# Attention products on four column tiles in a decoder block, and self maxima over 32 queries of four chunks

## The chip, the cores and the metric

The program runs on one core of one Trainium2 chip. The metric is the device time of one execution in microseconds (us), the median of some runs. TensorE (PE in the profile) multiplies; its weight loads are listed as PEld. VectorE is DVE, ScalarE is ACT, GpSimd is POOL, and SP only issues transfers.

## What is computed

A pre-norm decoder block on `x` of 4 x 1024 tokens with 256 features: windowed self attention (16 heads of 16, chunks of 128 queries that see their own chunk causally and the whole chunk before), cross attention over 77 context rows, and a gated layer with fake quantized operands.

```python
x = x + _L0_attn_ref(_layernorm(x, axis=-1), L0_attn_w_qkv, L0_attn_w_out)
x = x + _L0_xattn_ref(_layernorm(x, axis=-1), ctx_1024, ctx_1024, mask_SxS2_ik0, ...)
x = x + _L0_ffn_ref(_layernorm(x, axis=-1), L0_ffn_clip_x, ...)
```

Inside the self attention (`k_prev` of the first chunk is zeros, and those keys are masked out):

```python
scores = jnp.einsum('bhcqd,bhckd->bhcqk', qc, kcat) / HD ** 0.5
causal = wq[:, None] + W >= jk[None, :]
scores = jnp.where(mask[None, None], scores, -jnp.inf)
attn = jax.nn.softmax(scores, axis=-1)
```

## The kernel before

The attention is cut into 16 jobs (four batches x self `s` or cross `x` x half of the heads), each of two groups `g` of four heads: 32 groups. Jobs alternate along the list `JOBS`. All engines walk one list of steps, `attention_order()`: the steps of several jobs are interleaved by a table of places (`PLACE`, fractions of a group's length `LENGTH`) and by how many steps a follower stands behind (`BEHIND`). The order is fixed when the program is built, and the change leaves it as it is. A step uses one or two of six PSUM banks in a ring (`banks_of`); PE waits at a step until the engine that reads the banks' former content is done. Two more banks, `acc`, take the value products.

The steps, by the names that the diff uses:

- `turned`: eight transposes of normalized tokens (`xn`, f32), to `xnT` by ACT.
- `qk`: queries (z = 0) and keys (z = 1) of 512 tokens, f32. ACT and DVE split them into three bf16 parts, and SP copies the parts to `qs` and `ks` (96 rows: six products of parts for 16 features).
- `v` and `xkeys`: values of self and cross attention, f32.
- `max`: raw scores with the queries as weights, so that DVE can take each query's maximum over the keys (`tensor_reduce` with negation into `mneg`). For self attention a step is one chunk `c` of 128 queries against 256 keys (the chunk before and its own), four heads, and a product with `identb` and `causal` adds the mask. A group has eight such steps; for c = 0 there are only 128 keys. For cross attention a step is two chunks against 77 keys, with `maskq` as the mask.
- `rows` and `turnm`: DVE splits the maxima into three bf16 rows, PE transposes them, ACT copies them out (`m3t`) and sends them into rows 96 to 98 of `qs`, where the score product subtracts them.
- `score`: the scores again with the keys as weights, 128 keys by up to 256 queries, 99 rows; ACT takes the exponential into `pt`, and for self attention POOL zeroes what is not causal.
- `val`: values as weights (17 columns: 16 features and a one for the sum), f32, four heads side by side on four column tiles of 32, before and after the change.
- `out`: the output projection, f32.

An f32 matmul of the program stands twice in the trace: it is run as two.

From about 735 us on the gated layer runs, with full-width products; it is not touched.

The lines of the full-width products that the change replaces are L610, L630, L640, L649, L667 and L670 (self maxima), L677 and L679 (cross maxima), L687, L699 (self scores), L706 and L709 (cross scores), and L759. Transposes (L589, L595, L618, L771, L776) stay full width. L737 and L748 are the value products.

## Time and profile before

| | before |
|---|---|
| median of three runs | 855.02 us (847.9 to 858.87) |
| span of the profiled execution | 849.0 us |
| PE busy | 684.6 us, 5391 matmuls |
| DVE busy | 545.8 us |
| ACT busy | 415.1 us |
| POOL busy | 188.8 us |
| granted TensorE clock, mean over the span | 0.91 |

The profiled execution is one execution; its span, from the first to the last instruction, stands beside the runs' median, which is 6.0 us more. Busy times are shares of that span; PE's include the modelled latency of each matmul, so that what PE really does in a stretch is better read from the starts of its matmuls. A row of the timeline merges like instructions that follow each other: its first number is the start of the first, the second the time in which they are busy, and the count stands at the end. A matmul's form, such as 96*128 96x256 bf16, says 96 rows and 128 columns of weights, and 256 columns streamed.

### The profile page before, as it was taken

Reading aid. Unit: us, or ns where it says so; the run is one execution under the profiler, and the core shown is the slowest. Engines: PE = TensorE matmul, PEld = TensorE weight load, DVE = VectorE, ACT = ScalarE, POOL = GpSimd, SP = SyncE. Lnnn points to the kernel's source line nnn. Section 1 sums busy time; section 2 is a strip of 40 time slices with the busy share of each in tenths; the row PEclk is TensorE's granted clock in tenths of the full one; section 3 lists DMA queues with packets and bytes.
Section 4 is the critical chain, followed back from the end, with each engine's and each line's share of the span. In section 5 each row is a group of like instructions: output and inputs, shape, how many; then the busy total and the mean of one; then the engine's idle time right before and its main releaser. Section 6 shows DMA issues by size and latency. Waiting matters only on the chain.

```text
span 849.0 us, 14814 instructions
## 1 busy us (share of the span) xinstructions
PE 684.6 (81%) x5391; PEld 414.9 (49%) x5396; DVE 545.8 (64%) x975; ACT 415.1 (49%) x610; POOL 188.8 (22%) x231
## 2 busy tenths in 40 slices
PE   2579999989996998999979989897886784488565
PEld 1346565655653564556644644464543442233254
DVE  6277658866864456677636874556745651679996
ACT  2324665536463444555334446433343352399775
POOL 5002131312231120310113123002002000044436
PEclk9988999999997997999988989997998786699989
DMA  7534243502622153243222432331237112000013
GB/s 215 125 106 143 54 128 81 149 3 90 165 77 61 21 170 105 46 141 78 86 50 96 109 96 69 97 95 42 70 85 211 23 42 53 0 1 2 0 65 135
DMA packets 59557, 71.83 MB, mean 85 GB/s; under 512 B 25003, under 2 KB 36447, under 8 KB 59487
## 3 DMA queue, kind: packets, MB, share of 16 engines
q1 hardware_dynamic: 53391, 68.01, 29.2%
q10 hardware_dynamic: 6096, 2.88, 1.3%
q8 instruction: 44, 0.72, 0.4%
q14 instruction: 26, 0.21, 0.1%
HBM read 17.74 MB, written 4.72 MB: 26 GB/s over the span
## 4 chain that ended last, share of the span: by engine, by line
PE 49%; DVE 22%; issue 8%; ACT 7%; SPq 6%; DMA 6%; ACTq 1%; POOL 1%; POOLq 0%; DVEq 0%
PE banks L630 8%; PE banks L759 7%; PE banks L667 5%; PE banks L737 5%; DVE mneg L1179 4%; PE banks L699 4%; PE banks L640 3%; PE banks L748 3%; SPq L523 3%; PE banks L670 3%; DVE xn L1143 2%; SPq L517 2%; PE banks L706 2%; PE banks L709 2%; DVE tops L1358 2%
## 5 line engine op out<-in xcount | busy, mean ns | idle before, releaser
L1179 DVE TENSOR_REDUCE mneg<-banks 128x4 f32<-128x1024 f32 (+1 forms) x128 | 145.1, 1151 | 68.0 <-PE banks L670 67.5
L974 ACT ACTIVATE big<-banks 128x1024 f32<-128x1024 f32 (+1 forms) x128 | 123.0, 974 | 105.4 <-PE banks L699 101.7
L1451 POOL TENSOR_SCALAR_AFFINE_SELECT big<-big 128x512 f32<-128x512 f32 x128 | 83.1, 650 | 391.6 <-ACT big L974 390.9
L978 ACT ACTIVATE big<-banks 77x1024 f32<-77x1024 f32 x64 | 65.3, 1020 | 86.3 <-PE banks L709 81.8
L667 PE MATMUL banks<-big 96*128 96x256 bf16 (+1 forms) x512 | 94.5, 280 | 13.4 <-DMA big<-parts 9.8
L630 PE MATMUL banks<-xnT,weights 128*128 128x512 f32 x192 | 92.9, 617 | 3.9 <-ACT big L978 3.9
L699 PE MATMUL banks<-big 99*128 99x256 bf16 (+1 forms) x512 | 79.3, 280 | 13.3 <-DMA big<-m3t 5.7
L1183 DVE TENSOR_REDUCE mneg<-banks 128x8 f32<-128x616 f32 x64 | 50.3, 793 | 57.7 <-PE banks L679 57.6
L737 PE MATMUL banks<-big 128*17 128x256 f32 (+1 forms) x1152 | 79.0, 366 | 1.0 <-POOL big L1451 0.6
L670 PE MATMUL banks<-causal,identb 128*128 128x256 bf16 x256 | 72.9, 288 | 0.0
L667 PEld LDWEIGHTS banks<-big 96*128 96x128 bf16 x512 | 47.9, 103 | 45.9 <-issue 26.6
L699 PEld LDWEIGHTS banks<-big 99*128 99x128 bf16 x512 | 45.0, 101 | 48.3 <-issue 32.5
L803 PE MATMUL banks<-oe,weights 128*128 128x512 bf16 x187 | 46.8, 394 | 11.0 <-DVE big L1352 4.4
L630 PEld LDWEIGHTS banks<-xnT,weights 128*128 128x128 f32 x192 | 35.7, 197 | 38.1 <-issue 31.4
L677 PE MATMUL banks<-big 96*128 96x77 bf16 x512 | 43.1, 214 | 13.2 <-DMA big<-kparts 9.6
L706 PE MATMUL banks<-big 99*77 99x256 bf16 x256 | 51.1, 282 | 3.1 <-DVE big L1169 1.1
L677 PEld LDWEIGHTS banks<-big 96*128 96x128 bf16 x512 | 35.3, 108 | 32.9 <-issue 19.8
L709 PE MATMUL banks<-maskt,identb 77*77 77x512 bf16 x128 | 50.4, 394 | 0.0
L987 ACT COPY oe<-banks 128x512 f32<-128x512 f32 x64 | 37.2, 585 | 26.8 <-DMA oTx<-oe 10.9
L1224 DVE TENSOR_TENSOR xs<-banks,xs 128x512 f32<-128x512 f32 x32 | 22.1, 689 | 37.6 <-PE banks L759 37.6
L618 PE MATMUL banks<-ident,xn 128*128 128x128 f32 x128 | 23.7, 319 | 23.9 <-DVE xn L1143 23.5
L748 PE MATMUL banks<-big 77*17 77x256 f32 x512 | 42.7, 426 | 0.0
(155 smaller groups left out, 1163.8 us busy)
## 6 DMA issues: line engine op xcount, KB each, us to landing
big<-parts SPq DMA_DIRECT2D x282, 128.0 KB, 2.5
oc<-sums SPq DMA_DIRECT2D x16, 512.0 KB, 4.6
oTs<-oe SPq DMA_DIRECT2D x64, 64.0 KB, 2.3
out_dram<-oTs SPq DMA_DIRECT2D x16, 256.0 KB, 2.1
xs<-in_x_dram SPq DMA_DIRECT2D x3, 1024.0 KB, 5.8
big<-oe SPq DMA_DIRECT2D x32, 64.0 KB, 2.3
oTx<-oe SPq DMA_DIRECT2D x32, 64.0 KB, 2.3
big<-kparts SPq DMA_DIRECT2D x96, 9.6 KB, 1.8
```

What stands on the lines that cost most here:

```text
L630: t = e.matmul(bank(p), w[:, i, :], xnT[T][:, i, blk * 512:blk * 512 + 512], start=(i == 0), stop=(i == 1))
L667: e.matmul(bank(p, j)[:, i * 256 + lo * 128:i * 256 + 256], Q[0:96, hh, c * 128:c * 128 + 128], K[0:96, hh, (c - 1 + lo) * 128:(c + 1) * 1 ...
L670: t = e.matmul(bank(p, j).rearrange("p (s n) -> p s n", s=2)[:, :, 128:256], identb[:, :], causal[:, :].rearrange("p (a n) -> p a n", a=1) ...
L677: e.matmul(bank(p, j)[:, i * KX:i * KX + KX], Q[0:96, i, (c + j) * 128:(c + j) * 128 + 128], xks[r][0:96, i, :], start=(i == 0), stop=Fals ...
L699: t = e.matmul(bank(p, i // 2)[:, (i % 2) * 256:(i % 2) * 256 + n], ks[r][0:99, i, j * 128:j * 128 + 128], qs[r][0:99, i, j * 128:j * 128 ...
L706: e.matmul(bank(p, z)[0:KX, i * 256:i * 256 + 256], xks[r][0:99, 2 * z + i, :], qs[r][0:99, 2 * z + i, j * 256:j * 256 + 256], start=(i == ...
L709: t = e.matmul(bank(p, z)[0:KX, :].rearrange("p (i n) -> p i n", i=2), identb[0:KX, 0:KX], keep.to_broadcast([KX, 2, 256]), start=False, s ...
L737: t = e.matmul(acc[:, col // 512][32 * i:32 * i + 17, col % 512:col % 512 + z - a], va[f][:, j, 4 * g + i, :], P[:, i, a:z], start=new, st ...
L748: t = e.matmul(acc[:, j // 2][32 * i:32 * i + 17, (j % 2) * 256:(j % 2) * 256 + 256], xv[r][0:KX, i, 0:17], pt[u][0:KX, i * 256:i * 256 + ...
L974: e.activation(pt[u].rearrange("p (i n) -> p i n", i=4)[:, :, 0:n], pair(p).rearrange("p j (s n) -> p (j s) n", s=2)[:, :, 0:n], ACT.Exp, ...
L1179: e.tensor_reduce(M.rearrange("p (h c) -> p h c", h=4)[:, :, c], pair(p).rearrange("p j (s n) -> p (j s) n", s=2)[:, :, lo * 128:256], AX. ...
L1451: e.affine_select(out=P[:, :, 0:128], in_=P[:, :, 0:128], compare_op=ALU.is_ge, fill=0.0, base=0, pattern=[[0, 4], [1, 128]], channel_mult ...
```

## The change

Every product of the attention is issued as strips. A new helper cuts the weights into pieces of 32 columns and issues one matmul for each, with the same moving operand, on column tile 0, 32, 64 or 96, into the same 32 partitions of the bank as before. Only real transposes keep the full width. The transpose of the maxima (`turnm`) is now three strips with f32 output.

```diff
+            def strips(to, k, q, start, stop, w=128):
+
+                for u in range(0, w, 32):
+                    z = min(u + 32, w)
+                    t = e.matmul(to[u:z], k[:, u:z], q, start=start, stop=stop, tile_position=(0, u), skip_group_check=True)
+                return t
+
...
-                        t = e.matmul(bank(p), w[:, i, :], xnT[T][:, i, blk * 512:blk * 512 + 512],
-                                     start=(i == 0), stop=(i == 1))
+                        tokens = xnT[T][:, i, blk * 512:blk * 512 + 512]
+                        if kind == "s" and z == 0:
+                            tokens = tokens.rearrange("p (t a b) -> p a t b", t=4, a=4)
+                        t = strips(bank(p), w[:, i, :], tokens, i == 0, i == 1)
...
-                        lo = 1 if c == 0 else 0
+                        G, a = divmod(c, 4)
+                        own = 32 * a + 32
                         for j in range(2):
                             for i in range(2):
                                 hh = 2 * j + i
-                                e.matmul(bank(p, j)[:, i * 256 + lo * 128:i * 256 + 256], Q[0:96, hh, c * 128:c * 128 + 128],
-                                         K[0:96, hh, (c - 1 + lo) * 128:(c + 1) * 128], start=(i == 0), stop=False,
-                                         skip_group_check=True)
-                            t = e.matmul(bank(p, j).rearrange("p (s n) -> p s n", s=2)[:, :, 128:256], identb[:, :],
-                                         causal[:, :].rearrange("p (a n) -> p a n", a=1).to_broadcast([128, 2, 128]),
-                                         start=False, stop=True, skip_group_check=True)
+                                for u in range(4):
+                                    q = Q[0:96, hh, c * 128 + 32 * u:c * 128 + 32 * u + 32]
+                                    to = bank(p, j)[32 * u:32 * u + 32, i * 256:i * 256 + 128 + own]
+                                    k0 = (4 * G + u) * 128
+                                    if k0:
+                                        e.matmul(to, q, K[0:96, hh, k0 - 128:k0 + own], start=(i == 0), stop=False,
+                                                 tile_position=(0, 32 * u), skip_group_check=True)
+                                    else:
+                                        e.matmul(to[:, 0:128], q, K[0:96, hh, 0:1].to_broadcast([96, 128]), start=(i == 0),
+                                                 stop=False, tile_position=(0, 0), skip_group_check=True)
+                                        e.matmul(to[:, 128:128 + own], q, K[0:96, hh, 0:own], start=False, stop=False,
+                                                 tile_position=(0, 0), skip_group_check=True)
+                            for u in range(4):
+                                late = causal[:, 32 * u:32 * u + 32].rearrange("p (s n) -> p s n", s=1)
+                                t = e.matmul(bank(p, j)[32 * u:32 * u + 32, :].rearrange("p (s n) -> p s n", s=2)[
+                                    :, :, 96 + own:128 + own], identb[:, 32 * u:32 * u + 32], late.to_broadcast([128, 2, 32]),
+                                    start=False, stop=True, tile_position=(0, 32 * u), skip_group_check=True)
...
-                        lo = 1 if c == 0 else 0
                         e.tensor_reduce(M.rearrange("p (h c) -> p h c", h=4)[:, :, c],
-                                        pair(p).rearrange("p j (s n) -> p (j s) n", s=2)[:, :, lo * 128:256], AX.X, ALU.max,
-                                        negate=True).then_inc(d_max, 1)
+                                        pair(p).rearrange("p j (s n) -> p (j s) n", s=2)[:, :, 0:160 + 32 * (c % 4)],
+                                        AX.X, ALU.max, negate=True).then_inc(d_max, 1)
```

The second part of the change is in the maxima of self attention. The queries are stored in another order inside each half of 512 tokens: first queries 0 to 31 of the four chunks, then 32 to 63, and so on. Step `c` is quarter a = c mod 4 of the queries of four chunks; tile u holds those of chunk 4G + u, and its moving operand is that chunk's own stretch of keys. A quarter needs only 128 + 32 (a + 1) keys: 160, 192, 224 or 256. Only the last 32 of them need the mask, so the mask product streams 2 x 32 columns in place of 2 x 128. The very first chunk has no chunk before it; there tile 0 repeats one key 128 times and then takes its own keys. The scores read the queries through a rearranged address pattern, so that `pt` is as before:

```diff
+                            to = bank(p, i // 2)[:, (i % 2) * 256:(i % 2) * 256 + 256]
+                            k = ks[r][0:99, i, j * 128:j * 128 + 128]
+                            q = qs[r][0:99, i, :].rearrange("p (g a u b) -> p g u a b", g=2, a=4, u=4)
+                            G, u = divmod(j, 4)
+                            if u < 3:
+                                t = strips(to, k, q[:, G, u:u + 2, :, :], i % 2 == 0, True)
+                            else:
+                                t = strips(to[:, 0:128], k, q[:, G, 3, :, :], i % 2 == 0, True)
+                                if G == 0:
+                                    t = strips(to[:, 128:256], k, q[:, 1, 0, :, :], False, True)
```

`keys`, `v`, `xkeys`, `out`, the cross maxima and the cross scores are changed only by calling `strips` in place of `e.matmul`. PE gets 14,700 matmuls and as many loads in place of 5,396 each. The order of steps, the waits, the banks and the instructions of the other engines stay as they are, but for the reduction's width and the source format of the copy to `m3t`.

On PE, early in the program, the last self step of maxima of a group is followed by two pairs of a score step and a value step. Names: `big` holds queries, keys, values and exponentials. Before:

```order
L667 MATMUL banks<-big 128x256 x2
L670 MATMUL banks<-causal,identb 128x2x128
L699 MATMUL banks<-big 128x256 x4
L737 MATMUL banks<-big 17x256 x4
L699 MATMUL banks<-big 128x256 x4
L737 MATMUL banks<-big 17x128 x8
```

At the same place after the change:

```order
L680 MATMUL banks<-big 32x256 x8
L689 MATMUL banks<-causal,identb 32x2x32 x4
L579 MATMUL banks<-big 32x256 x16
L760 MATMUL banks<-big 17x256 x4
L579 MATMUL banks<-big 32x256 x16
L760 MATMUL banks<-big 17x128 x8
```

The steps stand in the same order. L667, L670 and L699 have become strips of 32 columns of weights, four for each product, and the mask's strips stream 2 x 32 columns. The value products (L737, now L760) are as they were, and nothing of full width stands between them any more.

On PE where the first cross job's maxima and scores meet the self values, before:

```order
L737 MATMUL banks<-big 17x128 x4
L706 MATMUL banks<-big 77x256 x2
L709 MATMUL banks<-maskt,identb 77x512
...
L677 MATMUL banks<-big 128x77 x4
L679 MATMUL banks<-maskq,identb 128x308
L640 MATMUL banks<-weights,xnT 128x128 x8
L667 MATMUL banks<-big 128x128 x2
```

After:

```order
L760 MATMUL banks<-big 17x128 x4
L579 MATMUL banks<-big 32x256 x2
L579 MATMUL banks<-big 13x256
L579 MATMUL banks<-maskt,identb 32x512 x2
L579 MATMUL banks<-maskt,identb 13x512
...
L579 MATMUL banks<-big 32x77 x16
L579 MATMUL banks<-maskq,identb 32x308 x4
L579 MATMUL banks<-weights,xnT 32x128 x32
L683 MATMUL banks<-big 32x128
L685 MATMUL banks<-big 32x32
L680 MATMUL banks<-big 32x160 x3
```

No full-width product is left between the value step and the next one; 77 keys make strips of 32, 32 and 13 columns, and the first step of self maxima has tile 0's two matmuls (L683, L685) beside the three of the other tiles.

## Rows read from the trace of the kernel before

**Rows 1.** The page's first part: busy us (share), instructions of each engine

```profile
PE 684.6 (81%) x5391; PEld 414.9 (49%) x5396; DVE 545.8 (64%) x975; ACT 415.1 (49%) x610; POOL 188.8 (22%) x231
```

**Rows 2.** Two stretches: busy us of PE, PEld, DVE, ACT, POOL; PEclk, DMA, GB/s

```profile
50.00:100.00 50.00, 42.69 (x316) 26.38 (x315) 37.69 (x67) 22.74 (x36) 8.42 (x12) 0.93 0.29 90
...
300.00:350.00 50.00, 45.24 (x385) 28.50 (x378) 34.40 (x65) 21.93 (x31) 10.71 (x13) 0.90 0.42 113
```

**Rows 3.** The page's chain that ended last, by engine

```profile
PE 49%; DVE 22%; issue 8%; ACT 7%; SPq 6%; DMA 6%; ACTq 1%; POOL 1%; POOLq 0%; DVEq 0%
```

**Rows 4.** The table of PE's waits: who waited, for whom, us, times, longest

```profile
PE banks L618 <- DVE xn L1143: 23.5, 19, 11.9
PE banks L759 <- DVE oTx L1216: 19.8, 3, 11.2
...
PE banks L667 <- DVE mneg L1179: 2.8, 7, 0.7
```

**Rows 5.** Timeline of PE: start us, us, line, matmul, out<-in, count

```profile
208.13 0.38 PE L667 MATMUL banks<-big 96*128 96x256 bf16 x2
208.36 0.27 PE L670 MATMUL banks<-causal,identb 128*128 128x256 bf16 x1
208.47 0.38 PE L667 MATMUL banks<-big 96*128 96x256 bf16 x2
208.69 0.27 PE L670 MATMUL banks<-causal,identb 128*128 128x256 bf16 x1
208.89 0.84 PE L737 MATMUL banks<-big 128*17 128x256 f32 x16
209.67 0.61 PE L699 MATMUL banks<-big 99*128 99x256 bf16 x4
```

**Rows 6.** Pieces of the chain in order of time: start us, us, what

```profile
94.32 3.44 PE banks L630 x8
...
114.14 1.79 PE banks L640 x16
...
185.39 1.76 PE banks L759 x8
```

**Rows 7.** Timeline of PE at 144 us

```profile
144.34 0.60 PE L699 MATMUL banks<-big 99*128 99x256 bf16 x4
144.87 0.63 PE L737 MATMUL banks<-big 128*17 128x256 f32 x8
145.43 0.35 PE L595 MATMUL banks<-ident,big 77*128 77x77 f32 x2
```

**Rows 8.** Timeline of PE at 207 us, a group's first step of maxima

```profile
207.24 0.28 PE L667 MATMUL banks<-big 96*128 96x128 bf16 x2
...
207.70 0.60 PE L699 MATMUL banks<-big 99*128 99x256 bf16 x4
```

**Rows 9.** Groups by shape: busy us, mean ns | idle before, and its releasers

```profile
L667 PE MATMUL banks<-big 96*128 96x128 bf16 x64 | 8.4, 225 | 9.8 <-DMA big<-parts 9.8
```

**Rows 10.** Timeline of PE at 353 us, maxima of cross attention

```profile
353.12 0.31 PE L677 MATMUL banks<-big 96*128 96x77 bf16 x4
353.27 0.30 PE L679 MATMUL banks<-maskq,identb 128*128 128x308 bf16 x1
```

**Rows 11.** PE's sequencer at L580 near 475 us: two waits, their starts

```profile
L580 PEldq EVENT_SEMAPHORE  x2: 51/51/51, 475.1 to 475.3; - x2
```

**Rows 12.** Groups by shape: the reduction of self attention's maxima

```profile
L1179 DVE TENSOR_REDUCE mneg<-banks 128x4 f32<-128x1024 f32 x112 | 134.1, 1218 | 41.9 <-PE banks L670 41.5
...
L1179 DVE TENSOR_REDUCE mneg<-banks 128x4 f32<-128x512 f32 x16 | 11.0, 686 | 26.0 <-PE banks L670 26.0
```

**Rows 13.** Weight loads: a stretch of the timeline, and two groups by line

```profile
299.83 0.13 PEld L737 LDWEIGHTS banks<-big 128*17 128x17 f32 x8 [0.57 <-POOL big L1451]
...
L640 PEld LDWEIGHTS banks<-weights,xnT 128*128 128x128 f32 x256 | 29.9, 192 | 1.2 <-issue 0.5 <-ACT big L978 0.5
...
L737 PEld LDWEIGHTS banks<-big 128*17 128x17 f32 x1152 | 22.1, 98 | 28.9 <-issue 21.2 <-POOL big L1451 4.4
```

More of the change, by code:

```diff
@@ L609, in run_tensor @@
                     for z in range(2):
-                        t = e.matmul(bank(p)[:, 0:NB * KX], xw[:, 0, z, f * 128:f * 128 + 128], ctxT[:, z, :],
-                                     start=(z == 0), stop=(z == 1))
+                        t = strips(bank(p)[:, 0:NB * KX], xw[:, 0, z, f * 128:f * 128 + 128], ctxT[:, z, :], z == 0, z == 1)
                     t.then_inc(t_keys, 1)
@@ L648, in run_tensor @@
                     for i in range(2):
-                        t = e.matmul(bank(p)[0:KX, 0:128], ctxT[:, i, b * KX:b * KX + KX],
-                                     xw[:, 1, i, f * 128:f * 128 + 128], start=(i == 0), stop=(i == 1))
+                        t = strips(bank(p)[0:KX, 0:128], ctxT[:, i, b * KX:b * KX + KX], xw[:, 1, i, f * 128:f * 128 + 128],
+                                   i == 0, i == 1, KX)
                     t.then_inc(t_xv, 1)
@@ L686, in run_tensor @@
                     e.wait_ge(d_rows, 4 * n_of["rows", job, g])
[L687 to L688 removed]
+                    strips(bank(p)[0:96, 0:128], m3[:, i, :, :].rearrange("p t n -> p (t n)"), identb[:, :], True, True, 96
+                           ).then_inc(t_turnm, 1)
                 elif k == "score":
@@ L758, in run_tensor @@
                         for f in range(2):
-                            t = e.matmul(bank(p)[:, i * 256:i * 256 + 256],
-                                         oT[kind][f][:, (c + i) * 128:(c + i) * 128 + 128],
-                                         wo[:, f, :] if kind == "s" else xw[:, 3, f, :], start=(f == 0), stop=(f == 1))
+                            t = strips(bank(p)[:, i * 256:i * 256 + 256], oT[kind][f][:, (c + i) * 128:(c + i) * 128 + 128],
+                                       wo[:, f, :] if kind == "s" else xw[:, 3, f, :], i == 0 and f == 0, f == 1)
                     t.then_inc(t_out, 1)
```

31 lines of the change are left out of this document (11 added, 20 removed).

## Prediction

> **What bounds the kernel now.** I read four views. The page's busy times put TensorE (PE) first: 684.6 of 849.0 us, VectorE (DVE) 545.8, ScalarE 415.1 [rows 1]. PE's ends are modelled, so the stretches are the second view: inside the attention, 50 to 100 us and 300 to 350 us, PE is busy 43 to 45 us of 50, DVE 34 to 38, ACT 22 to 23 [rows 2]. The chain that ended last is PE for 49% and DVE for 22% of the span [rows 3]. The table of waits says what PE waits for: mostly things that no product of the attention decides (the normalized tokens 23.5 us, the division by the sums 19.8), and for the maxima's reduction 2.8 us [rows 4]. So from about 20 to 700 us PE's own stream sets the pace, with idle places in it whose length hangs on DVE and on DMA chains. The rest, the gated layer from about 735 us, isn't touched.
>
> The fourth view is the timeline of PE, and it shows what the stream loses. A product starts 0.11 us after the one before it (208.36 to 208.47). At 208.69 the last full-width product starts, and the value products, which already run on column tiles, start at 208.89: 0.20 later in place of 0.11. Their 16 matmuls end with the next full-width product at 209.67 [rows 5].
>
> **What a change of mode costs.** Steady full-width f32 matmuls take 0.43 us for 512 columns (8 in 3.44), 0.22 for 256 (8 in 1.76) and 0.112 for 128 (16 in 1.79) [rows 6]. The 16 tile matmuls are four rounds of four tiles: two rounds of 256 columns, two of 128. If a round cost what one full-width matmul costs, 208.69 to 209.67 would be 0.11 + 2 x 0.22 + 2 x 0.112 = 0.77 us. It is 0.98 [rows 5]. So going in and out costs 0.21 us together. In the order of the built programs tile work stands in 168 separate stretches before and in 41 after (what is left are the turns of tokens and weights). 127 x 0.21 = **27 us** less.
>
> A shorter stretch tells the mode from the rounds. At 144.34 four products of 0.11 start, the last at 144.67; a value step of two rounds of 256 columns starts at 144.87, and the next full-width matmul at 145.43 [rows 7]. 0.76 - (0.11 + 2 x 0.22) = 0.21 us: the same with two rounds as with four, so the 0.21 belongs to the change of mode, and a round of four tiles with four different moving operands costs what one full-width matmul costs, to within the rounding (0.01 over two rounds, 0.005 each). That is for f32 with 17 columns of weights; bf16 strips of 32 columns stand nowhere in the trace.
>
> The Trainium skill (TensorEngine Tiling, "Key Properties") says that changing the tiling mode drains TensorE. The trace agrees, at 0.21 us for both ways.
>
> **The maxima of self attention.** A step before is four products of 256 columns and two mask products of 256: 208.13 to 208.69 plus 0.11, 0.67 us [rows 5]. The first step of a group is shorter, 207.24 to 207.70, 0.46 [rows 8]. A group has 7 and 1 of them, 5.15 us; there are 16 groups (64 products of 128 columns, four to a group) [rows 9]. After, the four products have 160, 192, 224 or 256 columns, by the step. At 0.11 us for 256 columns that is 0.07 to 0.11, mean 0.093. The mask product has 64 columns. The nearest row is the product of 77 columns: four in 0.15, 0.037 each [rows 10], and I take this. A step is then 4 x 0.093 + 2 x 0.037 = 0.45, a group 3.6; 1.55 x 16 = **25 us** less. Tile 0's additional matmul in the first four steps (128 plus the rest instead of one) streams no more columns.
>
> **The strips themselves.** 3080 full-width matmuls become rounds of four (three for the 77 keys). From below: 0, the row just read. From above: the 0.005 us that the rounding leaves, 15 us in all. I take 1.5 ns, nearer to the measured nothing, **+5 us**. The 512 products of 77 columns are the tightest: their round needs eight instructions in 0.037 us. The feed: 28 instructions stand between two waits of the sequencer that start at 475.1 and 475.3 [rows 11], at most 0.3 us apart by the rounding and most likely 0.2, 7 ns each with the second wait in it; 8 x 5 to 7 ns is 0.04 to 0.056. That gives +1.5 to +10 us for 512; I take **+3**.
>
> The transpose of the maxima becomes three plain strips, so that it is no full-width stretch any more; that is in the 127. The permuted order of the queries changes only address patterns (runs of 32 elements): nothing is added on DVE, ACT, GpSimd or a DMA queue, and no wait. What a strip's last tile ends later (three starts) is hidden behind the ring of six banks.
>
> **DVE.** The reduction takes 1218 ns for 1024 elements and 686 for 512 [rows 12], 1.04 ns per element. After: 640, 768, 896, 1024, that is 819, 952, 1085, 1218. Per group 8.15 instead of 9.21 us; 17 us less busy in all. As DVE is not the bound I count it as nothing by itself, but it is what keeps the reduction from being late next: in 50 to 100 us DVE would be busy some 36 us of what is then a stretch of 45.
>
> **The sum.** PE's stream: -27 - 25 + 5 + 3 = -44 us. How much reaches the end? The idle places don't shrink, and those that end in a chain (sums through DRAM, tokens normalized on DVE, the landing of parts) grow when PE comes earlier. In the stretches PE is busy 85 to 90% of a stretch; the order of steps was placed for the old lengths. I take 80%: -35 us. 849.0 - 35 = 814 for the profiled execution. The median of the runs is 855.0, 6 above this span, so **820 us**. With all of it, and no cost of strips, 52 us: 803. With half of the 44: 833.
>
> **Rivals.**
> 1. *The feed of instructions becomes the bound (slower).* PE gets 29,984 instructions instead of 11,376; a round takes eight where a product took two. For: the densest long stream of the trace, the products of 77 columns, is a load and a matmul in 0.037 us [rows 10], 18.5 ns per instruction, and nothing faster is shown over a long stretch. At 18.5 ns a round is 0.148. Against my prices that is +57 for the 77-column products, +28 and +28 for maxima and masks, +20 for the self scores, +18 for cross scores and value tokens: 151, less the 52 saved, +99 on the stream. At 80% 849 + 79 = 928, run 934. It decides from about 12.5 ns per instruction (round 0.10: +32 for the 77-column products, +21 for maxima and masks, all that was to be saved). Against: 7 ns or so [rows 11]. Chance 0.10. The Trainium skill (Runtime: NRT & Kernel Launch, "Instruction fetch mechanics") names an issue floor of about 20 cycles per instruction. With the 1.2 GHz that it gives the sequencer (TensorE: Matmul & The Clock Gate, Part 1) that is 16.7 ns, an estimate, and it would be this rival; the trace disagrees [rows 11].
> 2. *The loads of the four tiles don't overlap (no change).* A load of 128 f32 columns takes 192 ns, of 17 columns 98 [rows 13], 0.85 ns per column: 27 for 32, 0.109 for four one after another. Products of 256 columns would still hide it, but the 77-column ones cost +37 us, the mask products stay at 0.109 and the maxima gain 2: -27 - 2 + 37 = +8, run 855 to 865. Against: eight tile loads are over in 0.13 us, each taking 0.098 [rows 13], so that their starts lie within 0.035. That is for 17 columns. Chance 0.09. The Trainium skill (TensorEngine Tiling, "Restrictions and Gotchas") says that column tiling shuts off the fast weight load, the reason to take this rival seriously.
> 3. *The stream gets shorter, and waits take its place (no change).* DVE is at three quarters of a stretch [rows 2] and the group's chain of rows, transpose and landing before the first score isn't shortened. If under 40% arrives: 838 to 850. Chance 0.12.
> 4. *bf16 strips run at less than four tiles' rate* (all four read the same moving data), half rate being the price: all bf16 rounds double, over +100 us. Against: f32 tiles move 256 columns of 4 bytes in 0.22 us, as many bytes a ns as bf16 at 0.11 [rows 5, 6]. Chance 0.04, slower.
>
> **How the numbers follow.** My forecast, 800 to 838: 0.62; below 800: 0.03. Faster by over 2% (under 838; 2% is about what a measurement of this kernel can tell from no change) is their sum, 0.65. Within 2%: rivals 2 and 3, 0.21. Slower: rivals 1 and 4, 0.14. The range 800 to 860 takes in the forecast and rivals 2 and 3 but for the last us of rival 2, and leaves out what lies below 800 and rivals 1 and 4, under 0.2. The likeliest case alone has 800 to 838.
>
> **What would show it.** Right: full-width matmuls are gone from the attention but for transposes; a mask product starts 0.04 us before the next product; a maximum's step starts its first and last product within 0.45 us; value products follow a score product after 0.11, not 0.20; the reduction's mean is 1.02 us; PE's busy share in the two stretches falls little while they hold more steps. Wrong: rounds of 256 columns over 0.12 us apart, rounds of 77 columns over 0.06, PE idle with "issue" as the cause, or a table of waits in which the reduction or the normalized tokens have grown by tens of us. The prediction falls if PE's stream didn't set the pace, or if a round costs over 10 ns more than a product.

## The result, and the profile after

The changed kernel takes 858.4 us (median of 18 runs) against 851.9 us of the kernel before in the same series: a ratio of 1.0084, with a 95% interval from 1.0052 to 1.0117. The forecast was 820 us. The change makes the kernel slightly slower, by less than the 2% that the prediction calls no change. The profiled execution has a span of 862.0 us, 13.0 above the one before, and a granted clock of 0.893 over the span, against 0.911. The ratios leave out the runs that are over 1.5% longer than the fastest of their kernel, and the profiled execution of the changed kernel is such a run, the longest (864.2 us), so that the 13.0 us between the spans are twice the 6.5 between the medians.

The page of the changed kernel: PE's busy time, the instruction queue of PE with its packets, MB and share, and the chain that ended last by engine.

```profile
PE 648.7 (75%) x14695; PEld 426.3 (49%) x14700; DVE 527.6 (61%) x975; ACT 414.4 (48%) x610; POOL 189.4 (22%) x231
...
q8 instruction: 117, 1.92, 0.9%
...
PE 44%; DVE 18%; SPq 12%; issue 10%; ACT 7%; DMA 6%; POOL 1%; ACTq 1%; POOLq 0%; DVEq 0%
```

The same queue on the page of the kernel before:

```profile
q8 instruction: 44, 0.72, 0.4%
```

PE is busy 36 us less than in [rows 1] and the end is later: what was taken from the stream came back as idle time of PE. In the chain PE fell from 49 to 44%, DVE from 22 to 18%, while SP's queue rose from 6 to 12% and "issue" from 8 to 10% [rows 3]. The instruction queue's packets went from 44 to 117.

The two stretches of [rows 2], with the same columns:

```profile
50.00:100.00 50.00, 40.84 (x1002) 29.80 (x993) 35.11 (x67) 22.52 (x35) 8.32 (x12) 0.83 0.30 91
...
300.00:350.00 50.00, 40.76 (x1142) 30.21 (x1142) 32.27 (x65) 22.54 (x32) 11.90 (x15) 0.90 0.45 125
```

PE's busy share fell from 43 and 45 us to 41, and DVE does no more work per stretch than before. A stream that had only become shorter would show the same share of PE and more DVE work in 50 us.

PE's waits after (for [rows 4]): who waited, for whom, us, times, longest:

```profile
PE banks L624 <- DVE xn L1165: 25.8, 17, 12.4
PE banks L579 <- issue: 20.1, 19, 3.2
PE banks L579 <- DMA big<-kparts: 19.3, 4, 7.2
PE banks L579 <- DVE oTx L1237: 18.0, 3, 10.3
...
PE banks L683 <- DMA big<-parts: 12.6, 2, 8.7
...
PE banks L680 <- issue: 7.8, 5, 3.7
...
PE banks L579 <- DVE mneg L1204: 4.1, 2, 3.4
```

The same table of the kernel before, with the waits for parts and kparts, the longest wait for the cross maxima's reduction (`mneg`), and "issue":

```profile
PE banks L667 <- DMA big<-parts: 9.8, 2, 8.8
PE banks L677 <- DMA big<-kparts: 9.6, 2, 4.9
...
PE banks L677 <- DVE mneg L1183: 3.4, 1, 3.4
PE banks L699 <- issue: 3.3, 1, 3.3
```

"Issue" means that PE waited for nothing that the profile shows. It grew from 3.3 to 28 us in these rows. Waits for the landing of queries and keys (parts, kparts) grew from 19.4 to 31.9. The waits that the prediction read as the ones a faster PE would stretch hardly moved (xn 23.5 to 25.8, oTx 19.8 to 18.0).

**What stopped PE.** Three places of the timeline of PE after (start us, us, line, operation, out<-in, count; in brackets the idle time ahead and its cause):

```profile
161.24 1.04 PE L579 MATMUL banks<-weights,xnT 128*32 128x128 f32 x31
162.10 0.61 PE L579 MATMUL banks<-big 99*32 99x128 bf16 x29
163.90 0.23 PE L579 MATMUL banks<-big 99*32 99x128 bf16 x3 [1.19 <-issue]
...
218.31 0.38 PE L680 MATMUL banks<-big 96*32 96x256 bf16 x5 [0.40 <-ACT big L996]
...
222.43 0.40 PE L680 MATMUL banks<-big 96*32 96x256 bf16 x3 [3.73 <-issue]
```

PE stops in the middle of a step, where the program has no wait: after 29 of 32 products of a score step, and at 218.3 after 5 of 8 products of a maximum's two heads. Beside the second stop the instruction queue moves one packet (a fetch), from 219.67 for 1.26 us; PE goes on 1.5 us after its end. PE's loads and products can be counted from the first on. Of the pauses over 0.25 us from one product's start to the next that end 1.0 to 1.75 us after a fetch's end, 25 come ahead of an instruction whose number leaves 193 or 194 when divided by 256 (a few records are missing), and no other remainder has more than two. These are the stops at a page's edge, 25 of them, 30.5 us in all. (A pause of 3.7 us at 620.5, near the same remainder, is not one: it ends with DVE's reduction, and the kernel before has the same wait of 3.4 us.) The 117 packets have 16 KB each, 64 bytes for each of 256 instructions, and 117 x 256 is 29,952 of PE's 29,984. So PE's program comes in pages of 256 instructions, and PE stops where the next page isn't there. In the kernel before no remainder stands out: its fetches start at least 9.2 us apart. After, none starts sooner than 3.3 us behind the one before, with many at 3.6 to 3.8. That is 13 to 15 ns per instruction. The steps of the changed kernel want more within a page: a self maximum has 48 instructions or a few more in 0.35 to 0.50 us (7 to 11 ns each), a cross maximum 80 in 0.58 us (7 ns), a self score or value step 32 in 0.44 us (13.7 ns).

Pace alone doesn't explain every stop. Ahead of the one at 218.7 PE goes past a page's edge at 214.68 and uses the next 256 instructions by 218.7, without a long pause; the fetch before this one had started at 212.30, yet the next starts only at 219.67, 5.0 us after the edge. Over the 25 stops a fetch starts 1.1 to 5.4 us after PE has gone past the edge before, and from that edge to the stop's end it is 3.7 to 7.8 us, over 4.3 us in 16 of them. What makes a fetch start late isn't shown by any run here.

The Trainium skill (Runtime: NRT & Kernel Launch, "Instruction fetch mechanics") has the same blocks of 256 instructions, which the sequencer fetches over a DMA queue of its own, and calls the crossing of a block's edge mostly hidden. The trace agrees with the blocks; the 25 stops show where hiding ends.

### The profile page after: what moved, and what is told of

Same layout as the page of the kernel before. It is cut to its first block, busy times and chain, and to the rows that moved or that the text cites. A ratio compares the mean times of both kernels' runs of the same rounds, so it can differ in the third digit from the quotient of the medians.

```text
span 862.0 us, 33422 instructions
## 1 busy us (share of the span) xinstructions
PE 648.7 (75%) x14695; PEld 426.3 (49%) x14700; DVE 527.6 (61%) x975; ACT 414.4 (48%) x610; POOL 189.4 (22%) x231
## 4 chain that ended last, share of the span: by engine, by line
PE 44%; DVE 18%; SPq 12%; issue 10%; ACT 7%; DMA 6%; POOL 1%; ACTq 1%; POOLq 0%; DVEq 0%
PE banks L579 29%; SPq L517 5%; SPq L523 4%; PE banks L760 3%; PE banks L680 3%; PE banks L771 3%; ACT big L996 2%; DVE mneg L1200 2%; SPq L535 2%; DVE tops L1379 2%; PE banks L624 2%; DVE xn L1165 2%; DMA oc<-sums 2%; DVE big L1373 1%; PE banks L825 1%
## 5 line engine op out<-in xcount | busy, mean ns | idle before, releaser
L579 PE MATMUL banks<-big 96*32 96x77 bf16 (+3 forms) x5120 | 188.2, 251 | 54.7 <-DMA big<-kparts 19.3
L579 PEld LDWEIGHTS banks<-big 99*32 99x32 bf16 (+2 forms) x5120 | 129.3, 103 | 108.5 <-issue 71.8
L1200 DVE TENSOR_REDUCE mneg<-banks 128x4 f32<-128x640 f32 (+3 forms) x128 | 128.1, 1017 | 81.9 <-PE banks L689 77.4
L579 PE MATMUL banks<-xnT,weights 128*32 128x512 f32 x768 | 96.4, 616 | 6.3 <-ACT big L1000 5.8
L680 PE MATMUL banks<-big 96*32 96x160 bf16 (+3 forms) x1792 | 84.9, 271 | 14.5 <-issue 7.8
L760 PE MATMUL banks<-big 128*17 128x256 f32 (+1 forms) x1152 | 79.9, 361 | 2.0 <-POOL big L1472 1.4
L680 PEld LDWEIGHTS banks<-big 96*32 96x32 bf16 x1792 | 50.9, 103 | 27.4 <-issue 14.5
L689 PE MATMUL banks<-causal,identb 128*32 128x64 bf16 x1024 | 61.2, 204 | 0.8 <-issue 0.8
L579 PE MATMUL banks<-maskt,identb 77*32 77x512 bf16 (+1 forms) x384 | 55.4, 410 | 1.3 <-issue 1.3
L1009 ACT COPY oe<-banks 128x512 f32<-128x512 f32 x64 | 37.2, 583 | 34.6 <-DMA oTx<-oe 13.5
L683 PE MATMUL banks<-big 96*32 96x128 bf16 x256 | 39.9, 239 | 14.6 <-DMA big<-parts 12.6
L579 PE MATMUL banks<-maskq,identb 128*32 128x308 bf16 x512 | 46.9, 338 | 0.0
L624 PE MATMUL banks<-ident,xn 128*128 128x128 f32 x128 | 25.0, 336 | 25.8 <-DVE xn L1165 25.8
```

The lines of the kernel that those rows point to most:

```text
L579: t = e.matmul(to[u:z], k[:, u:z], q, start=start, stop=stop, tile_position=(0, u), skip_group_check=True)
L680: e.matmul(to, q, K[0:96, hh, k0 - 128:k0 + own], start=(i == 0), stop=False, tile_position=(0, 32 * u), skip_group_check=True)
L689: t = e.matmul(bank(p, j)[32 * u:32 * u + 32, :].rearrange("p (s n) -> p s n", s=2)[:, :, 96 + own:128 + own], identb[:, 32 * u:32 * u + 3 ...
L760: t = e.matmul(acc[:, col // 512][32 * i:32 * i + 17, col % 512:col % 512 + z - a], va[f][:, j, 4 * g + i, :], P[:, i, a:z], start=new, st ...
L1200: e.tensor_reduce(M.rearrange("p (h c) -> p h c", h=4)[:, :, c], pair(p).rearrange("p j (s n) -> p (j s) n", s=2)[:, :, 0:160 + 32 * (c % 4)],
```

## The experiments

The theories: **A**, the pages bound the dense stretches; **B**, waits for DVE, ACT and transfers take the gain, whatever the number of instructions. Later **D**: fetches slow SP's issues and so the landing of queries and keys. "Stops" below are those at a page's edge, counted as above in each run's profiled execution (those that the table of waits puts down to another engine are left out). "Stream" is PE's work without waits: each kind of step at its shortest tenth from start to start at full clock, summed over all steps of the attention; 505 us before, 444 after. The ratios compare with the kernel before in the same series; they are better compared with each other than the times, since the kernel before itself has medians from 848.4 to 852.7 us in the series of the experiments.

**Parts of the change undone.** First the value tokens at full width again, then the cross maxima as well (with their mask products):

```diff
-                            t = strips(bank(p)[:, (c - c0) * 128:...], xnT[0][:, i, c * 128:c * 128 + 128], wqkv[...], ...)
+                            t = e.matmul(bank(p)[:, (c - c0) * 128:...], xnT[0][:, i, c * 128:c * 128 + 128], wqkv[...], ...)
```

```diff
-                                strips(bank(p, j)[:, i * KX:i * KX + KX], Q[0:96, i, (c + j) * 128:...], xks[r][0:96, i, :], ...)
+                                e.matmul(bank(p, j)[:, i * KX:i * KX + KX], Q[0:96, i, (c + j) * 128:...], xks[r][0:96, i, :], ...)
```

> The changed kernel with the value products of the tokens (v) at full width again. Theory A, instructions are fetched in pages of 256 and a page can't be used up in less than about 3.8 us: the strips of a v step are one page in 1.8 us, so 6 of 117 fetches go, and the stalls at v with them; 15 more changes of mode cost 3 us. 848 to 855 us. Theory B, PE's stream got shorter as forecast but waits on DVE and on SP's queue of transfers took its place, and the fetch is no matter: 858 to 862, the changes of mode added.

> As before, and the maxima of cross attention at full width too. Theory A: 96 fetches in place of 117, and the densest stretches after the self maxima are gone; 59 more changes of mode than the changed kernel has cost 12 us of stream; 838 to 850 us, faster than both kernels. Theory B: only the changes of mode are added, 862 to 870.

Measured: 854.5 us, ratio 1.0074 (1.0032 to 1.0116), and 852.6 us, 1.0059 (1.002 to 1.0098). The profiled execution of the first took 1237.7 us, for a reason that isn't known; it is left out. With both parts undone there are 96 fetches, and 8 stops of 11.4 us in all instead of 25 of 30.5, although 59 switches came back and the stream is 9 us longer. Neither ratio is clear of the changed kernel's 1.0084, so the first run decides nothing. The second speaks against B, which had 12 us added (a ratio of some 1.022); but A had the kernel faster than both others, and it is slower than the kernel before.

**The strips without the new maxima, and the new maxima without the strips.** The first has the old four products of 256 columns and the old order of queries on strips; the second keeps the new order, the four-chunk maxima and the shorter reduction, and makes the helper a plain product:

```diff
             def strips(to, k, q, start, stop, w=128):
-                for u in range(0, w, 32):
-                    ...
+                return e.matmul(to, k[:, 0:w], q, start=start, stop=stop, skip_group_check=True)
```

> Everything on strips, but the self maxima, their reduction and the order of queries as in the kernel before. PE's stream is 25 us longer than in the changed kernel, DVE 17 us busier; 113 fetches in place of 117. Theory A: the page's time, not the columns, bounds the dense stretches, so a good part of the 25 us is hidden in stalls that get shorter: 858 to 866. Theory B with waits for DVE as the filler: 862 to 875. If neither, and PE's stream is the bound: 875 or more.

> Only the self maxima in the new form on tiles (with the value products as before); everything else at full width. 65 fetches, 205 stretches of tile work (37 more than the kernel before, 8 us). Theory A: few stalls, the 25 us of shorter maxima arrive less 8 and less what waits take: 835 to 845. Theory B: the gain is taken by waits: 850 to 860.

Measured: 858.7 us, 1.0104 (1.0059 to 1.0148), for the strips alone; 842.8 us, 0.9976 (0.9934 to 1.0019), for the maxima alone. The strips alone cost what the whole change costs. Their stream is 26 us longer than the changed kernel's (470.8 against 444.4); against that stand fewer stops (14, 16.6 us, against 25, 30.5), other waits, and in the profiled executions a higher clock (0.903 against 0.893). The new maxima alone are clearly faster than the changed kernel, but not clearly faster than the kernel before. A second series of that kernel:

> The new self maxima alone once more (all else of full width, as before), with more rounds, since 842.8 us with a ratio of 0.9976 and the interval 0.9934 to 1.0019 left open whether any of the 25 us of shorter maxima reach the end. If the profile's 11.5 us are real: ratio 0.985 to 0.995. If waits take what the shorter maxima save: 0.996 to 1.003.

Measured: 843.3 us, 0.9943 (0.9901 to 0.9984). The two series together put the new maxima alone 2 to 5 us ahead of the kernel before (by their medians 6), of the 25 that the prediction priced for the maxima.

**More instructions, the same columns.** Each product of the self maxima is cut in two by columns, in the changed kernel and in the kernel before:

```diff
-                                        e.matmul(to, q, K[0:96, hh, k0 - 128:k0 + own], ...)
+                                        w = 64 + own // 2
+                                        e.matmul(to[:, 0:w], q, K[0:96, hh, k0 - 128:k0 - 128 + w], ...)
+                                        e.matmul(to[:, w:2 * w], q, K[0:96, hh, k0 - 128 + w:k0 + own], ...)
```

```diff
-                                e.matmul(bank(p, j)[:, i * 256 + lo * 128:i * 256 + 256], ..., K[0:96, hh, (c - 1 + lo) * 128:(c + 1) * 128], ...)
+                                for y in range(lo, 2):
+                                    e.matmul(bank(p, j)[:, i * 256 + y * 128:i * 256 + y * 128 + 128], ..., K[0:96, hh, (c - 1 + y) * 128:(c + y) * 128], ...)
```

> The changed kernel with each product of the self maxima cut in two by columns: the same columns, 14 pages of 256 instructions more in the program, all of them where it is densest. Theory A (PE gets its instructions in pages of 256, a page no sooner than 3.3 to 3.8 us after the one before, so about 14.5 ns per instruction over a longer stretch): the self maxima's steps get 28 to 32 instructions more each, 0.4 us of feed, hidden only where PE waits anyway; 875 to 905 us, more stops in the middle of steps than the 26 of the changed kernel. Theory B (an instruction costs nothing as long as the columns cover it, 7 ns at most; what was lost was lost to waits for DVE and transfers): 858 to 868 us.

> The control: the kernel before with each 256-column product of its self maxima cut into two of 128, 7 instructions in place of 5 per bank. Theory A: this stream needs a page every 9 us or so, far from 3.7, so the cut costs nothing of the feed: 847 to 853 us, no stop at a page's edge. A cost of 14.5 ns per instruction everywhere (theory C) would give +13 us: 859 to 865. Theory B: 847 to 853.

Measured: 889.1 us, 1.0485 (1.0409 to 1.0562), for the cut of the changed kernel; 846.2 us, 0.9981 (0.9939 to 1.0024), for the cut of the kernel before. PE's waits in the first:

```profile
PE banks L579 <- issue: 27.2, 20, 4.3
...
PE banks L681 <- issue: 9.7, 10, 1.9
PE banks L683 <- issue: 9.1, 8, 3.3
...
PE banks L692 <- issue: 3.7, 3, 1.7
```

The rows have 50 us of "issue" where the changed kernel has 28. There are 41 stops, 55.9 us, and 131 fetches; the stream is the same (445.4 us). In the kernel before there are 48 fetches at least 6 us apart, no stop, and no cost. The same kind of cut costs 4% where instructions are dense and nothing where they are not. This refutes a fixed price per instruction, and B as an account of what dense instructions cost; waits of B's kind remain beside the stops (see the mix below).

**The feed by itself.** Behind the end of the kernel before, PE runs products whose results nobody reads:

```diff
+            e.wait_ge(f_y, 16)
+            for n in (64, 128, 256):
+                for r in range(192):
+                    for u in range(4):
+                        e.matmul(bank(0)[32 * u:32 * u + 32, 0:n], identb[:, 32 * u:32 * u + 32], xb[:, 0:n], ..., tile_position=(0, 32 * u))
+            for n in (32, 64, 128):
+                for r in range(768):
+                    e.matmul(bank(0)[:, 0:n], identb[:, :], xb[:, 0:n], ...)
```

> The kernel before with additional products behind its end whose results nobody reads: three series of 192 rounds on four column tiles (64, 128 and 256 columns, 8 instructions a round) and three of 768 full-width products (32, 64 and 128 columns, 2 instructions each), 1536 instructions a series, all bf16, no waits between. Theory A: 14 to 15 ns per instruction wherever the columns ask for less: rounds of 64, 128 and 256 columns all at 0.112 to 0.12 us, full-width products of 32 and 64 columns at 0.029, of 128 at 0.055. Theory B: rounds at 0.03 to 0.056, 0.056 and 0.11 us, products at 0.014 to 0.02, 0.028 and 0.055.

The timeline of PE in these series, one execution:

```profile
845.72 1.60 PE L829 MATMUL banks<-oc,identb 128*32 128x64 bf16 x173 [2.22 <-POOL oTs L1508]
849.83 1.38 PE L829 MATMUL banks<-oc,identb 128*32 128x64 bf16 x128 [2.52 <-issue]
853.84 1.90 PE L829 MATMUL banks<-oc,identb 128*32 128x64 bf16 x128 [2.62 <-issue]
857.84 1.90 PE L829 MATMUL banks<-oc,identb 128*32 128x64 bf16 x128 [2.11 <-issue]
...
876.48 1.97 PE L829 MATMUL banks<-oc,identb 128*32 128x128 bf16 x128 [0.92 <-issue]
879.93 1.97 PE L829 MATMUL banks<-oc,identb 128*32 128x128 bf16 x128 [1.48 <-issue]
883.39 1.97 PE L829 MATMUL banks<-oc,identb 128*32 128x128 bf16 x128 [1.49 <-issue]
...
890.60 20.18 PE L829 MATMUL banks<-oc,identb 128*32 128x256 bf16 x723 [1.13 <-issue]
...
919.15 3.35 PE L833 MATMUL banks<-oc,identb 128*128 128x32 bf16 x128 [0.41 <-issue]
922.89 3.35 PE L833 MATMUL banks<-oc,identb 128*128 128x32 bf16 x128 [0.39 <-issue]
```

PE works in bursts of 128 products with their loads, 256 instructions, and then stops. A page of 128-column tile products is over in 1.97 us, 7.7 ns an instruction (what the prediction had read), but the pages start 3.45 us apart (876.48, 879.93, 883.39), 13.5 ns an instruction. With 64 columns, at the lower level of the clock for most of the time (0.50 in 853 to 866 us), the pages start 3.7 to 4.0 us apart, no closer than with 128. Of the rounds only those of 256 columns soon run without a stop, at 20.18 / 723 = 0.028 us per product. In a long stream a round of four tiles costs 0.11 to 0.125 us however few columns it has, near A's figures; so do full-width products of 32 columns, 0.029 us each (919.15 to 922.89 for 128).

The fetches beside these bursts show what a page's period is made of. A fetch starts 1.0 to 1.3 us after PE has gone past a page's edge, lasts 0.9 to 1.4 us, and PE goes on 1.2 to 1.6 us after its end: 3.45 to 4.0 us together. So in these series the next page is asked for only once PE has entered the page ahead of it, and a page that is used up sooner than that ends in a stop.

**A mix with fewer strips.** The new maxima, the self scores, the turn of the maxima and the keys on tiles, the rest of full width: 131 stretches of tile work and 79 fetches.

```diff
-                        t = strips(bank(p), w[:, i, :], tokens, i == 0, i == 1)
+                        t = wide(bank(p), w[:, i, :], tokens, i == 0, i == 1)
```

(and so for the value tokens, cross maxima, cross scores and outputs; wide is one plain product).

> The new self maxima, the self scores, the turn of the maxima and both kinds of keys on tiles, everything else (queries and keys of self, value tokens, cross maxima and scores, outputs) of full width: 131 stretches of tile work against 205 with the new maxima alone, 168 before and 41 after, and some 80 fetched pages against 65, 44 and 117. Theory A: switching falls by 74 x 0.21 = 16 us against the new maxima alone (842.8), a few us of stops at page edges come back: 828 to 838 us. Theory B (waits for DVE, transfers and queues take whatever the stream saves): 840 to 850 us.

Measured: 854.5 us, 1.0092 (1.0047 to 1.0138). A miss for A: the stream is shorter than with the maxima alone by the 16 us expected (490.7 to 474.2), and the kernel 11 us slower. Seven stops of 7.2 us (three of 1.9 with the maxima alone) don't explain that. The timeline of SP shows a second thing. With the maxima alone, ahead of the first cross maximum:

```profile
237.03 8.33 SPq L523 DMA_DIRECT2D big<-parts  x12
245.46 5.32 SPq L517 DMA_DIRECT2D big<-kparts  x6
250.88 2.50 SPq L535 DMA_DIRECT2D oTs<-oe  x4
253.48 0.53 SPq L542 DMA_DIRECT2D sums<-ls  x1
254.10 3.78 SPq L517 DMA_DIRECT2D big<-kparts  x6
```

In the mix:

```profile
243.82 9.70 SPq L523 DMA_DIRECT2D big<-parts  x12
253.62 6.59 SPq L517 DMA_DIRECT2D big<-kparts  x6
260.31 2.43 SPq L535 DMA_DIRECT2D oTs<-oe  x4
262.85 0.53 SPq L542 DMA_DIRECT2D sums<-ls  x1
263.47 3.77 SPq L517 DMA_DIRECT2D big<-kparts  x6
```

SP issues 29 transfers nearly without a pause, and PE waits for the landing of the last six, 6.2 us with the maxima alone and 9.1 in the mix. The same 29 take 20.9 us in the first and 23.4 in the second. The single issues say where that comes from: nearly all last 0.6 us, and those that overlap a fetch of PE's instructions 0.9 to 1.2 us on average (0.60 for the others, in every run). In the attention 34 of SP's issues meet a fetch before, 62 and 57 in the two profiles of the maxima alone, 71 in the mix, 106 after. From the maxima alone to the mix that is only some ten issues more, so D can explain no more than a part of the 11 us.

**Is it the fetch that slows an issue?** 120 small transfers by SP behind the end of the kernel before, the first part beside a dense series of PE:

```diff
+            for n in range(120):
+                e.dma_start(xks[0][n % 6:96:6, :, :], kparts[0:64, 0, K_PART[n % 6], 0:KX]).then_inc(land_s[0], 16)
+                if n % 6 == 5:
+                    e.wait_ge(land_s[0], 16 * (len(JOBS) + n + 1))
```

> The kernel before with, behind its end, a dense series of tile products (448 rounds of 64 columns, 14 pages of PE's instructions, no waits) beside 120 small transfers that SP issues one by one, the first half of them beside the series, the rest with PE idle. Theory D: an issue that meets a fetch lasts 1.0 to 1.2 us, the others 0.6, and with PE idle all last 0.6; the series itself again at 27 to 30 ns per product with its load. If an issue's length follows the data traffic instead: no difference between the two halves.

One issue beside a fetch (853.40, 1.43 us), and four with PE idle:

```profile
853.31 1.91 SPq L567 DMA_DIRECT2D big<-kparts  x1
...
901.71 2.46 SPq L567 DMA_DIRECT2D big<-kparts  x4
```

One execution: 17 issues overlap a fetch, mean 0.85 us, up to 1.91 (16 while PE's series runs, and one of 1.30 just behind it). The others take 0.59 us, beside the series as with PE idle, and with PE idle none of those 70 is longer than 0.60. So an issue that meets a fetch is longer, by less than D's figure on average, and not each one is. The series itself ran at 28.8 ns per product with its load.

**Is that what the end lacks?** The 12 transfers of a cross job's keys are issued by GpSimd, in place of SP, in the kernel with the new maxima alone and in the changed kernel:

```diff
+                if k == "bulk" and s[1][0] == "x" and s[3] == 1:
+                    ...
+                    for rr in range(6):
+                        e.dma_start(xks[r][rr:96:6, :, :], kparts[...]).then_inc(land_xk[r], 16)
```

> The new self maxima on tiles, the rest of full width, as in the run of the new maxima alone (842.8 us), and the 12 transfers of a cross job's keys issued by GpSimd in place of SP. Theory D (the gain is partly lost because PE waits at a job's first maximum for queries and keys that SP issues one by one, 0.6 us each and 1.0 to 1.2 where a page of PE's instructions is fetched meanwhile; 19 us of waits with the new maxima, 11 before): 7 us of SP's queue are gone in front of each cross job's first maximum, 8 to 10 us of the end: 831 to 836. If the wait only moves to something else, or GpSimd's own issues hold up the masking that stands in its order: 841 to 850.

> The changed kernel with the same move of the cross keys' transfers to GpSimd. Theory D: 24 us of such waits, of which some 10 to 13 go: 845 to 850. The stops at page edges stay as they are, 20 to 30 of them, since PE's program is the same. If the page edges take up what is saved (PE comes earlier to the next page): 853 to 860.

Measured: 854.4 us, 1.002 (0.9976 to 1.0065), and 861.1 us, 1.0143 (1.0073 to 1.0213). Both missed D's figures. PE's wait for the keys is as long as before the move: in the first of the two kernels

```profile
261.51 0.42 PE L574 MATMUL banks<-big 96*128 96x77 bf16 x4 [5.89 <-DMA big<-kparts]
```

against 6.21 us at the same step with SP issuing. GpSimd starts the last six at 256.72, 1.1 us after PE has begun to wait, since they stand in its order behind the masking of the exponentials. So this move only exchanged one queue for another; how much of the end SP's slower issues cost isn't settled by it. In the changed kernel the stops stay, as expected: 19 of 23.2 us.

**Instructions without tiles.** The new maxima alone, with each full-width product of the self scores cut in four by columns:

```diff
+            def cut(to, k, q, start, stop):
+                for y in range(4):
+                    t = e.matmul(to[:, y * w:y * w + w], k, part(q, y), start=start and y == 0, stop=stop)
```

> The new self maxima on tiles as in the run of them alone (843 us), the self scores still of full width but each product cut in four by columns: the same number and places of instructions as with the self scores on tiles (69 pages against 70), the same columns, and all 205 stretches of tile work, so no switch saved. Theory D (what undoes the saved switches of the self scores on tiles is the number of instructions: stops at page edges, and SP's issues that meet a fetch): 850 to 862 us, ratio 1.003 to 1.015. Theory E (it is the faster stream itself, which meets waits for the exponentials, the masking and the transfers): 842 to 847, ratio 0.993 to 0.999.

Measured: 851.3 us, 1.0038 (1.0 to 1.0075), inside D's figures, but the profile shows another cost. In its profiled execution (a span of 857.0 us, one of the longest runs) 11 us more than with the maxima alone lie in the score steps themselves, above all those with two ranges of queries, whose products have only 32 columns: 0.885 us in place of 0.541. In the series above a full-width product of 32 columns takes 26 ns (3.35 us for 128), while a product of 128 takes 56 ns there, so that its columns ask for 14. This price of short products wasn't foreseen, and it hides what the 78 fetches cost (five stops of 4.8 us); the run doesn't tell D from E.

What the mix loses therefore stays open in part. By the trace, against the maxima alone, where PE is idle: 5 us more at page edges, 5 for queries and keys, 11 for exponentials, masking and the reduction of maxima, and the clock takes 6 (0.897 against 0.903, and 147 against 133 us at the lower level in the attention). These are 27 of the 33 us that stand against the 16 saved (the two profiled executions lie 16 us apart, the medians 12). But the profile of the maxima alone that is used here is of one of its shortest runs. In the profile of its second series, 846.4 us long, PE waits 30.2 us for queries and keys, against 27.0 in the first and 31.9 in the mix. So part of these differences is what two executions of one kernel differ by, and which wait causes which was not separated.

## Why the prediction was wrong, step by step

- **The mode's price was right.** Value products follow a mask product without the 0.20 us of [rows 5], and strips run at the round's price. In the timeline after (the rows from 208.11 on are of a window that opens behind the first two value products):

```profile
208.07 0.20 PE L689 MATMUL banks<-causal,identb 128*32 128x64 bf16 x3
208.10 0.40 PE L760 MATMUL banks<-big 128*17 128x256 f32 x3
...
208.11 0.85 PE L760 MATMUL banks<-big 128*17 128x256 f32 x14
208.76 0.64 PE L579 MATMUL banks<-big 99*32 99x256 bf16 x16
```

208.76 to the next step's first product at 209.20 is 0.44 us for 16 strips, four rounds of 256 columns at 0.11. The mix has 74 switches fewer than the maxima alone and a stream shorter by 16.5 us, 0.22 each.
- **The maxima's price was right.** Steps with 160, 192, 224 and 256 columns take 0.35, 0.39, 0.45 and 0.50 us, mean 0.43 where 0.45 was taken. The reduction's mean is 1.02 us (1017 ns), as forecast.
- **Products of 77 columns** take 0.15 us for four rounds, as they did for four products [rows 10]:

```profile
358.88 0.34 PE L579 MATMUL banks<-big 96*32 96x77 bf16 x16
359.03 0.33 PE L579 MATMUL banks<-maskq,identb 128*32 128x308 bf16 x4
```

- **The stream's sum** was forecast at -44 us and is -60.6 by the steps' shortest tenths. Eight of the 17 us between are the price of the strips (+5 and +3), which measured nothing; the rest isn't traced. The step that failed is not in this sum.
- **The step that failed is the feed.** "The strips themselves" took 28 instructions in 0.2 us [rows 11], 7 ns each, as the rate at which PE gets instructions. That is about right (7.7 ns in the series), but only inside a page that is already there. The rate over a longer stretch is a page in about 3.5 us, 14 ns each, and no row of the kernel before could show it, since its pages are at least 9 us apart. The prediction had no row over more than 28 instructions at that pace, and took a local rate for a lasting one: in its sum the feed is +3 us, and the stops at page edges alone are 30.5.
- **Rival 1 was right in kind and wrong in extent.** It priced 18.5 ns for every instruction of the dense kinds of steps, +99 us of stream. The limit is about 14 ns, and it holds over pages: where PE waits for something else, the next page comes meanwhile. So 30.5 us of stops came of it, not 99. Its point of decision, 12.5 ns, lies below what the series measured.
- **The share that arrives** was taken as 80%. In the two profiled executions +67 us of waits and +5 of clock stand against -60.6 us of stream. 30.5 us of the waits are stops at page edges. By PE's table 13 us are waits for queries and keys, which SP issues, 6 for DVE (76 to 82) and 6 for exponentials on ACT (8 to 14); some 12 are spread over many small ones. So the stops are the largest single item, and a little less than half. Rival 3 named waits that take the gain's place, but looked for them in DVE's chains, which grew by these 6 us alone.
- **The clock** is an item that no run separates. In the kernel before, 23 runs of one series go from 838.4 us at a granted clock of 0.928 to 859.5 at 0.889, and those with the lower clock are mostly the longer ones, some 6 us for 0.01. The changed kernel's 18 runs have 0.898 on average, the kernel before 0.908 to 0.912 in the series of the experiments. Whether the clock fell because PE stops more often, and how much of the 6.5 us is its doing, is not shown.
- **The range.** 858.4 us lies within 800 to 860, but by luck: its upper part was there for rivals 2 and 3, and rival 2 didn't happen, while rival 3's 838 to 850 was passed.
- **DVE** was rightly no bound. **Rivals 2 and 4** are refuted: rounds of 256 bf16 columns run at 0.11 us and rounds of 77 at 0.037.

## What to carry to other kernels

Before many small tile products replace few large ones, count instructions, not only columns: here PE needs at least some 14 ns per instruction over every stretch of more than a page or two (256 instructions, a product with its load being two), and more where a fetch starts late. The fetches show on the page of the profile as packets of the instruction queue. A stop of PE in the middle of a step, with "issue" as its cause and a multiple of 256 instructions behind the last one, is a missing page. Take the part of such a change that shortens products for few instructions (here the new maxima alone, 0.9976 and 0.9943), and leave saved switches of 0.21 us alone where they come with many instructions: here 127 switches for 73 pages, and 25 of the pages stopped PE for 1.2 us each.

## What the runs showed of the hardware

- PE's instructions arrive in pages of 256, no sooner than 3.3 us one after the other, 3.45 to 4.0 in steady series. Inside a page tile products with their loads start 15 ns apart (7.7 ns per instruction), full-width ones of 32 columns 26 ns apart.
- In the steady series the fetch of the next page starts 1.0 to 1.3 us after PE goes past an edge. Ahead of the changed kernel's stops it starts 1.1 to 5.4 us after it.
- An issue of SP that meets a fetch is longer: 0.85 us on average and up to 1.9, instead of 0.59, in the run made for it.
- A round of four bf16 strips of 32 columns of weights over 256 or 77 columns costs what one full-width product of as many columns costs.
